# Reordering half 1's FIR, products and recurrence around half 0's recurrence in a gated delta-rule block

## The reference

```
x = x + 0.5 * ffn(layernorm(x))
x = x + attention(layernorm(x))
x = x + 0.5 * ffn(layernorm(x))      # the same weights

def ffn(x):      # 128 -> 512 -> 512 -> 512 -> 128, per-channel scales
    h = silu(x @ w1.T * s1) * (x @ w2.T * s2)
    h = gelu(h @ h1.T * g1);  h = gelu(h @ h2.T * g2)
    return h @ w3.T * s3

def attention(hs):                   # 4 heads of 32 channels
    q, k, v = (silu(conv4(hs @ W)) for W in (Wq, Wk, Wv))
    beta = sigmoid(hs @ Wb)
    delta = delta_rule(q, k, v, beta)          # chunks of 32 tokens
    paths = [fir3(v), fir15(v), fir64(v), delta, v]
    stats = mean, mean square, mean |.|, norm of each path and head
    logits = gelu([hs, stats] @ gW1 + gb1) @ gW2 + gb2
    probs = softmax(logits / tau) * (1 - sum(eps)) + eps
    o = rmsnorm(sum(probs * paths)) * norm_w
    return o @ Wo

def delta_rule(q, k, v, beta):       # after l2norm of q and k
    T = inv(I + strict_lower(kb @ k.T));  u = T @ v_beta;  w = T @ kb
    for each of the 8 chunks:                  # state S, 32 x 32 a head
        u_i = u - w_i @ S
        o_i = q_i @ S + lower(q_i @ k_i.T) @ u_i
        S   = S + k_i.T @ u_i
```

## Time and profile before

| | us |
|---|---|
| median of 3 runs | 449.09 |
| lowest, highest | 447.48, 451.02 |
| the profiled execution | 447.03 |
| its span, first to last instruction | 445.3 |
| TensorE busy in it | 373.6 (84%) |
| VectorE busy | 295.2 (66%) |
| ScalarE busy | 277.3 (62%) |
| GpSimd busy | 42.2 (9%) |
| mean granted clock of TensorE | 0.892 of full speed |

### The profile page before, as it was taken

The page is one execution under the profiler, slowest core; times in us unless marked ns, Lnnn a source line. Parts: engine busy times, 40 slices in busy tenths (PEclk is TensorE's granted clock), DMA queues, the critical chain, the costliest instruction groups (busy, mean ns, idle before and its releaser), DMA issues.

```text
span 445.3 us, 9784 instructions
## 1 busy us (share of the span) xinstructions
PE 373.6 (84%) x4132; PEld 279.9 (63%) x4132; DVE 295.2 (66%) x461; ACT 277.3 (62%) x434; POOL 42.2 (9%) x103
## 2 busy tenths in 40 slices
PE   5599999999999998893995668843799687978996
PEld 3487776678866776793784666421266465556885
DVE  2896779538135757699774778297768696568533
ACT  4788948888597776381533107426477849458973
POOL 4000000000000100001888100000000000000000
PEclk9699999999999998697966575958889898989999
DMA  8900009300000000250430000070000000001001
GB/s 273 324 1 2 2 1 253 79 1 2 0 1 0 1 2 3 69 147 2 112 108 4 3 4 3 25 237 0 0 1 1 2 0 2 0 1 50 1 1 47
DMA packets 14325, 19.75 MB, mean 44 GB/s; under 512 B 960, under 2 KB 9152, under 8 KB 14272
## 3 DMA queue, kind: packets, MB, share of 16 engines
q1 hardware_dynamic: 14128, 18.94, 14.2%
q10 hardware_dynamic: 144, 0.01, 0.0%
HBM read 17.91 MB, written 1.05 MB: 43 GB/s over the span
## 4 chain that ended last, share of the span: by engine, by line
PE 53%; DVE 21%; POOL 7%; ACT 7%; issue 5%; DMA 4%; SPq 1%; DVEq 0%; ACTq 0%; POOLq 0%
PE ps_a L726 11%; PE ps_a L727 11%; PE ps_a L830 8%; POOL arena L464 4%; POOL arena L462 4%; PE ps_d L726 3%; PE ps_d L727 2%; DMA w_in<-in_w 2%; DVE arena L1077 2%; DVE arena L1074 2%; PE ps_a L920 2%; PE ps_d L861 2%; PE ps_a L918 2%; DMA w_in<-in_h 2%; DVE hbuf L1119 2%
## 5 line engine op out<-in xcount | busy, mean ns | idle before, releaser
L726 PE MATMUL ps_a<-acts,w_f 128*128 128x512 f32 x256 | 103.5, 404 | 8.6 <-ACT acts L600 8.5
L727 PE MATMUL ps_a<-acts,w_f 128*128 128x512 f32 x256 | 101.5, 396 | 0.0
L726 PEld LDWEIGHTS ps_a<-acts,w_f 128*128 128x128 f32 x256 | 49.2, 192 | 22.0 <-ACT acts L600 10.2
L727 PEld LDWEIGHTS ps_a<-acts,w_f 128*128 128x128 f32 x256 | 49.2, 192 | 10.8 <-issue 0.7
L600 ACT ACTIVATE acts<-ps_a,vec 128x512 fp32r<-128x512 f32 x64 | 44.6, 697 | 0.0
L830 PE MATMUL ps_a<-xnp,conv_w 128*128 128x512 f32 x156 | 38.5, 404 | 0.0
L1143 DVE TENSOR_TENSOR acts<-gbuf,acts 128x512 fp32r<-128x512 f32 x32 | 21.6, 688 | 24.9 <-ACT acts L600 24.9
L1143 DVE TENSOR_TENSOR acts<-ghbuf,acts 128x512 fp32r<-128x512 f32 x32 | 21.2, 689 | 20.8 <-ACT acts L600 20.8
L830 PEld LDWEIGHTS ps_a<-xnp,conv_w 128*128 128x128 f32 x156 | 29.2, 188 | 8.2 <-issue 1.4
L990 DVE SCALAR_TENSOR_TENSOR arena<-ps_d,arena 128x512 f32<-128x512 f32 x16 | 11.0, 687 | 30.4 <-ACT arena L554 26.3
L597 ACT ACTIVATE gbuf<-ps_a,vec 128x512 f32<-128x512 f32 x32 | 22.3, 696 | 10.1 <-PE ps_a L727 9.8
(11 more groups left out here) (211 smaller groups left out, 789.5 us busy)
## 6 DMA issues: line engine op xcount, KB each, us to landing
toep<-in_fir SPq DMA_DIRECT2D x24, 288.0 KB, 5.9
w_in<-in_h SPq DMA_DIRECT2D x4, 1024.0 KB, 8.5
g_rows<-in_gW SPq DMA_DIRECT2D x4, 640.0 KB, 6.8
w_in<-in_w SPq DMA_DIRECT2D x6, 256.0 KB, 4.4
iobuf<-in_x SPq DMA_DIRECT2D x4, 256.0 KB, 6.3
toep<-in_taps SPq DMA_DIRECT2D x1, 768.0 KB, 6.8
y<-iobuf SPq DMA_DIRECT2D x3, 256.0 KB, 2.3
toep<-in_proj SPq DMA_DIRECT2D x1, 256.0 KB, 8.7
```

The costliest lines, as they stand in the source:

```text
L726: e.matmul(bank, w, hi, start=start, stop=False)
L727: return e.matmul(bank, w, lo, start=False, stop=stop)
```

## The change

Only the list and what depends on it. FIR pieces 8 to 11 (in list order; the first four of half 1) go ahead of `yy` 0, and pieces 12 to 15 between the steps of half 0's recurrence. `xt` 1, `yy` 4 to 7 and `aq` 4 and 5 leave that recurrence and stand behind its `turn3`; `bo` 4 to 7 stand behind the logits, and half 1's recurrence runs between the pieces of the mixture, the RMS norm and the output product. Some statistics change places. Half 0's gate layer writes a buffer of its own (`hid0`), the logits and their transpose get other places in the arena. No instruction is added or dropped.

```diff
     s += [("token", 2, i) for i in (0, 1, 4, 5, 8, 9, 2, 3, 6, 7, 10, 11)]
-    s += [("window", 2, i) for i in range(8, 16)] + fir[4:8]
-    s += [("yy", 2, 0), fir[8], ("yy", 2, 1), fir[9], ("turn4", 2, 0), ("turn4", 2, 1), ("sq", 2, 0)]
-    s += [("yy", 2, 2), fir[10], ("sq", 2, 1), ("yy", 2, 3), fir[11]] + sums(0) + [("sq", 2, 2)] + sums(1)
-    s += [("sq", 2, 3), ("aq", 2, 0), fir[12], ("r1", 2, 2), ("aq", 2, 1), fir[13], ("r2", 2, 2), ("r3", 2, 2), ("sq", 2, 4),
-          ("aq", 2, 2), fir[14], ("r1", 2, 3), ("aq", 2, 3), fir[15], ("r2", 2, 3), ("r3", 2, 3)]
-    s += [("bo", 2, b) for b in range(4)] + [("sq", 2, 5)] + sums(4) + [("sq", 2, 6)]
-    ahead = [("xt", 2, 1)] + [("yy", 2, k) for k in range(4, 8)] + [("aq", 2, k) for k in range(4, 8)]
-    between = {1: [("r1", 2, 5)], 2: [("r2", 2, 5)], 3: [("r3", 2, 5)], 4: [("numbers", 2, 0)],
-               5: [("r1", 2, 6)], 6: [("r2", 2, 6)], 7: [("r3", 2, 6)]}
-    s += [("first", 2, 0)]
+    s += [("window", 2, i) for i in range(8, 16)] + fir[4:12]
+    s += [("yy", 2, k) for k in range(4)] + [("turn4", 2, 0), ("turn4", 2, 1), ("sq", 2, 0), ("sq", 2, 1)] + sums(0)
+    s += [("aq", 2, 0), ("r1", 2, 1), ("aq", 2, 1), ("r2", 2, 1), ("aq", 2, 2), ("r3", 2, 1), ("aq", 2, 3), ("sq", 2, 2),
+          ("bo", 2, 0), ("bo", 2, 1), ("sq", 2, 3), ("bo", 2, 2), ("bo", 2, 3)] + sums(2) + [("r1", 2, 3), ("first", 2, 0)]
+    beside = {1: [fir[12], ("r2", 2, 3)], 2: [fir[13], ("r3", 2, 3), ("sq", 2, 4)], 3: [fir[14], ("r1", 2, 4)],
+              4: [fir[15], ("numbers", 2, 0)], 5: [("r2", 2, 4)], 6: [("r3", 2, 4)], 7: []}
     for n in range(1, NCH):
-        s += [("rec", 2, n), ahead[n - 1]] + between[n]
-    s += [("turn3", 2, 0), ("sq", 2, 7), ("aq", 2, 6), ("aq", 2, 7), ("bo", 2, 4), ("bo", 2, 5), ("bo", 2, 6)]
-    s += sums(7) + [("turn", 2, 0), ("bo", 2, 7), ("sq", 2, 8), ("first", 2, 1), ("gate", 2, 0), ("gate", 2, 1)]
+        s += [("rec", 2, n)] + beside[n]
+    s += [("turn3", 2, 0), ("sq", 2, 5), ("xt", 2, 1)] + [("yy", 2, k) for k in range(4, 8)] + sums(5) + [("turn", 2, 0)]
+    s += [("sq", 2, 6), ("sq", 2, 7), ("aq", 2, 4), ("aq", 2, 5), ("gate", 2, 0), ("gate", 2, 1)] + sums(6) + sums(7)
+    s += [("aq", 2, 6), ("aq", 2, 7), ("sq", 2, 8), ("logit", 2, 0), ("logit", 2, 1), ("r1", 2, 8), ("r2", 2, 8)]
+    s += [("bo", 2, b) for b in range(4, 8)]
     half = [None] + [("rec", 2, NCH + n) for n in range(1, NCH)]
-    s += sums(8) + [half[1], ("logit", 2, 0), half[2], ("logit", 2, 1),
-                    ("lturn", 2, 0), half[3], ("soft", 2, 0), ("round", 2, 0), half[4], ("prob", 2, 0), ("mul", 2, 0),
-                    half[5], ("addmix", 2, 0), ("mul", 2, 1), ("add", 2, 1), ("osq", 2, 1),
-                    half[6], ("rms", 2, 0), half[7], ("scale", 2, 0), ("turn3", 2, 1), ("sq", 2, 9), ("wo", 2, 0), ("wo", 2, 1)]
+    s += [("lturn", 2, 0), ("soft", 2, 0), ("round", 2, 0), ("r3", 2, 8), ("prob", 2, 0), ("mul", 2, 0), ("first", 2, 1),
+          half[1], ("addmix", 2, 0), ("mul", 2, 1), half[2], ("add", 2, 1), ("osq", 2, 1), half[3], ("rms", 2, 0),
+          half[4], ("scale", 2, 0), half[5], ("wo", 2, 0), half[6], ("wo", 2, 1), half[7], ("turn3", 2, 1), ("sq", 2, 9)]
     s += sums(9)
...
-STATS = ((4, 0), (0, 0), (1, 0), (2, 0), (4, 1), (0, 1), (1, 1), (3, 0), (2, 1), (3, 1))
-LAST_STAT = (7, 9)
+STATS = ((4, 0), (0, 0), (1, 0), (2, 0), (4, 1), (3, 0), (0, 1), (1, 1), (2, 1), (3, 1))
+LAST_STAT = (5, 9)
...
-          sq=36864, st=34816, stt=4096, hid=6144, lg=8192, pl=10240, small=12288,
+          sq=36864, st=34816, stt=4096, hid=6144, hid0=16384, lg=18432, pl=4096, small=12288,
...
-        hid = at("hid", 2, 2, TILE)
+        hid = [at("hid0", 2, 2, TILE), at("hid", 2, 2, TILE)]
```

More of the change, by code:

```diff
@@ L671, in _ @@
                         e.wait_ge(S["pe_a"], a + m + 1)
-                        e.activation(hid[:, i % 2, m], ps_a[(a + m) % NRING][:, :], ACT.Gelu,
+                        e.activation(hid[i // 2][:, i % 2, m], ps_a[(a + m) % NRING][:, :], ACT.Gelu,
                                      bias=vc("gb1", m)).then_inc(S["act_a"], 1)
@@ L926, in _ @@
                         e.wait_ge(S["act_a"], A_AT[("gate", 2, i)] + m + 1)
-                        last = e.matmul(bank, gate_2[:, m, :], hid[:, i % 2, m], start=m == 0, stop=m == 1)
+                        last = e.matmul(bank, gate_2[:, m, :], hid[i // 2][:, i % 2, m], start=m == 0, stop=m == 1)
                     last.then_inc(S["pe_a"], 1)
```

## The result

The changed kernel takes 442.25 us (four runs, 440.14 to 442.51) beside 449.36 for the kernel before: ratio 0.984, 95% interval 0.981 to 0.987. The forecast was 441.0, with 436 to 446 around it. In the changed kernel's file lines stand three numbers lower: L1199 is L1196, L887 is L884, and so on.

A forecast was written before the change was run, and what follows sets the result against it. Two gates were taken as the bound: GpSimd's elimination for half 1, then the second layer's weight load and rounding. Half 1's gate layer moves from 322.31 to 314.9, 7.4 us earlier; from the 449.09 median 441.7, taken as 441.0, range 436 to 446.

The forecast's parts named there:

- part 4: Start of half 1's `xt` on VectorE: GpSimd's end at 246.5 still sets it, with 0.4 us of slack.
- part 5: From GpSimd's end to the logits: gates 0 and 1 take 6.2 us, logits end at 270.9, 16.5 earlier.
- parts 6 to 8: Logits to RMS reduce: weights rounded by 288.3, waits added at the exponential and step 10 (3.8 us), reduce at 295.2.
- Part 1: FIR pieces 8 to 11 fill TensorE's 7.00 us wait for half 0's `xt`: cost nothing, no DMA late.
- Part 2: Half 0's small products stand bare on TensorE, code blocks 3.63 us apart; first state turned at about 229.3.
- Part 3: Half 0's recurrence: FIR pieces between steps cover VectorE's 0.8 us; seven steps end at 244.2, `turn3` at 246.1.
- half 0's recurrence misses GpSimd: Rival: FIR and block entries make the seven steps 4 us later; 3 us gain left, 444 to 446; chance 0.17.
- Part 9: Tail from output product to half 1's gate layer: 13.7 us, before 10.3, so 3.4 given back.
- No limit by code loading: Rival: code blocks do not pace TensorE's small products; end 10.1 us earlier, 437 to 439; chance 0.20.
- That the edit does nothing: Rival: the weights' load sets the end, so the edit gains nothing, only if the logits do not move; chance 0.04.
- The slower case: Rival: TensorE stays at 1.2 GHz from `yy` 4 until the mixture is summed; price 15.2 us, so 457; chance 0.05.

The follow-up runs named there:

- front part alone: The kernel before with only FIR pieces 8 to 11 moved into TensorE's wait for the first `xt`: 448.89 us, ratio 1.000.
- back part alone: The changed kernel with half 1's FIR pieces put back between `yy` and `aq` of half 0: 449.86 us, ratio 1.003 to the kernel before.
- the exponential and `xt`: The changed kernel with the exponential ahead of `bo` 4 to 7's evictions (438.61 us), with half 1's `xt` ahead of `turn3` (440.15), and with both (438.13).

## Why the prediction was right

**Its frame held.** The front part alone gives nothing and the back part alone gives nothing, the two together do; the gate layer of half 1 moved by 6.4 us like for like where 7.4 was forecast, and the end by 6.0. The 1.0 between forecast and measured adds up from 2.6 lost in part 4, 1.8 won in part 5, 0.4 lost in parts 6 to 8 and 0.2 won in the rest.

**Part 1** (FIR 8 to 11 hidden): right for TensorE, whose `yy` 0 waited for `xt` and not for FIR. Its "no DMA is late" looked at the wrong party. The reloads were in time for their own readers, but they held up TensorE's code.

**Part 2** (products bare, paced by code blocks, first state at 229.3): the mechanism was right, the places of the stands too, and it kept the forecast from a further 2.7 us of gain that the same sum gives without it. Its size was off: 233.92, or 3.6 late after the 1.0 of the execution. Of that 2.9 to 3.2 is the reloads, shown by leaving them out; the remainder is that blocks followed at 3.5 to 3.9 us even without them, and not at 3.63 throughout.

**Part 3** (half 0's recurrence): 14.3 us from the first state to the last step's addition at 248.2, forecast 14.9. A FIR piece between two steps covers VectorE's share: the first five steps followed each other at 2.1 to 2.6 us.

**Part 4** (GpSimd's 246.5 stays the start of `xt` 1, slack 0.4): this step failed. The recurrence ended 0.8 us behind GpSimd and `turn3` put in another 1.9, so `xt` began 2.6 behind GpSimd. That the slack was so small was seen, and priced as the rival "half 0's recurrence misses GpSimd". Its outcome came true in part, but not its mechanism: it put the lateness into the seven steps, which took less than forecast (part 3), while it came from part 2, the products' blocks behind the reloads. Without the reloads `xt` waited for GpSimd again. With `xt` ahead of `turn3` it began without a wait, 0.2 us behind GpSimd.

**Part 5** (GpSimd to logits): `turn0` was released by ScalarE's square root behind `yy` 7, with 3.64 us of VectorE idle ahead of it. From the start of `xt` 1 to the end of the logits it took 22.6, forecast 24.4: `yy` took 5.7 instead of 6.7 to 7.7, its last two products at the high clock (0.50 until 256, 0.97 over 256 to 258). It took 5.2 to 6.6 in the ten other kernels with the back part, so the forecast had this term too long. This repaid two thirds of what part 4 lost. Gates 0 and 1 ran at the high clock throughout, as forecast, but that was luck in part: in five of the ten other kernels with the back part the clock was low in a part of those gates, which cost 1.4 to 2.5 us.

**Parts 6 to 8**: the weights were rounded at 285.33 to 290.23, with the mixture sum done 2.4 behind them; the exponential stood behind `bo` 7; VectorE stood for step 10 for 3.73, forecast 3.8. From the end of the logits to the RMS reduce 24.7, forecast 24.3. Two experiments price the added waits at 3.0 for the exponential (forecast 2.4 bare) and 1.8 net for step 10. ScalarE's rows of the changed kernel, the rounding and the eviction of the mixture sum:

```profile
285.33 4.90 ACT L663 ACTIVATE w_f<-w_in 128x5632 fp32r<-128x5632 f32 x1 [3.56 <-DMA w_in<-in_w]
292.68 0.60 ACT L686 ACTIVATE arena<-ps_a 128x512 f32<-128x512 f32 x1 [2.45 <-PE ps_a L930]
```

**Part 9** (tail, 13.7 from the output product to the gate layer): 13.6.

**The rivals.** No limit by code loading is out: stretches of 127 matmuls with "issue" ahead of them stand in every profiled kernel but the back part alone, where FIR pieces lie between the products. That the edit does nothing is out too: the logits ended at 272.71 instead of 287.39, and the weights were rounded 14.6 us earlier. The slower case, TensorE at 1.2 GHz through the gates, did not come, but its weaker form, a part of gates 0 and 1 at the low clock, did in the profiles of five of the ten other kernels with the back part. On the code blocks, the Trainium skill's page "Advanced Engine Details and Errata", section ISA Cache, with its two lines of 256 instructions, agrees with the stands after 127 matmuls, which are 254 instructions with their weight loads. That DMA traffic lengthens them is shown by the runs: 5.35 us for a block in the changed kernel, 3.54 without the reloads.

## What to carry to other kernels

When work is moved into an engine's wait, look at what the moved work releases: here DMA reloads, which fell onto a stretch in which TensorE was paced by its code loads. Two moves can each be worth nothing and still pay together, when one makes room and the other gets a chain out from behind a gate (here another engine's elimination). In a list that orders all engines at once, each entry sets a place in every queue: the exponential behind four evictions and the recurrence step behind a long sum cost about 3 us each. Moving one entry took back 3.0 of the first, and 1.8 of the second once the step's own time behind it is counted.

## What the runs showed of the hardware

- A run of small fp32 matmuls (32x32 by 64 columns) stands every 127 of them, for 0.5 to 1.3 us in most cases, blocks of code following at 3.4 to 4.2 us. With the DMA engines full at about 260 GB/s it was 5.35 us, and 4.8 to 6.7 in the other kernels that keep the reloads.
- The granted clock of TensorE in the same stretch differs from kernel to kernel with an equal order in the stretch itself: gates 0 and 1 took 6.4 or 8.9 us, gates 2 and 3 5.9 or 7.6. Gains of 1.5 to 2 us ahead of such a stretch vanished in it in two profiles. Whether small gains add can hardly be told from the medians: the exponential and `xt` gave ratios of 0.977 and 0.982 by themselves and 0.977 together, and the intervals overlap.
- Two heads instead of four in a packed product did not halve its time: 128 matmuls in 3.2 us against 176 in 2.49, that is 25 ns each against 14 (one run; the reason was not tested).
